# Row maxima of an attention kernel: head start of one and three quarter units instead of two

## The chip, the cores and the metric

The kernel runs on one core of one Trainium2 chip. The metric is the device time of one execution in microseconds (us), lower is better; of several executions the median counts.

## The reference

What is computed is one layer of gated cross attention and a gated, fake-quantised feed-forward part, on x of shape (8, 512, 256):

```python
x = x + tanh(g_xattn) * attention(layernorm(x), ctx, ctx)     # 16 heads of 16, rope on q and k, softmax
x = x + tanh(g_ffn) * ffn(layernorm(x))                       # 704 inner columns, int8 fake quantisation
```

The attention is the part that matters here: for each of 8 batches and 16 heads, scores = q k^T / 4 over 512 queries and 512 keys, a softmax over the keys, and the weighted sum of v. The softmax subtracts each query's largest score before the exponential.

## The kernel before

The program has three stages: projections and rope (stage A), attention (stage B), feed-forward (stage C). Each is a block in which the five engines run their own instruction streams and wait for one another by semaphores. The change touches stage B alone.

**Units and key tiles.** In stage B the work is cut in 32 units: batch b (8) times a group g of 4 heads. A unit has 4 key tiles kt of 128 keys. For each key tile and head h, TensorE computes the scores transposed (128 keys by 512 queries, `scores`, L716, four matmuls side by side) into one of three PSUM banks `st_ps`, and ScalarE takes the exponential of the bank (`exps`, L857). After the 4 heads of key tile kt, TensorE multiplies the probabilities of key tile kt-1 with the values (`weigh`, L748). At the second key tile of the next unit VectorE turns the finished sums (`turn_out`, L924) and inverts the denominators (`invert_sums`, L930).

**The row maxima come first.** A query's largest score must be known before its exponentials. It enters the score matmul as two more rows of q (a bf16 value and its rest) against rows of ones in k, so that the matmul itself subtracts it. To get it, the scores are computed once more the other way round, ahead of time: `query_scores` (L724) fills a pair of banks `mx_ps` with two query tiles of one head (8 matmuls), and VectorE's `maxima` (L916) reduces the pair to two columns of `negm`. A unit has 8 such pairs, and there are two pair buffers in turn. `ahead_scores` puts one pair behind the first and one behind the third head of every key tile (L809 to L812); so unit u+2's eight pairs are spread over the four key tiles of unit u: head kt of that unit at key tile kt. The first two units have nothing ahead of them: their 16 pairs stand alone in a prologue (L827 to L842 on TensorE, L1028 to L1036 on VectorE).

**How a maximum gets into q.** When a unit's eight pairs are read (`mx_read`), GpSimd splits `negm` in two bf16 parts (`split_max`, L1084 and L1086); TensorE turns them (`max_transpose`, L758) into a bank of the `st_ps` ring; ScalarE copies that to `mrow` (`take_max`, L862); and SyncE's queue sends two DMAs of 4 KB (`max_rows`, L688) into the two extra rows of `q6[g]`. TensorE waits for `mrow_in[g]` at the start of the unit (L806). `max_transpose` for unit u+1 stands behind the first key tile (kt == 0) of unit u, and so does `take_max`. SyncE's queue works strictly in order: at each unit first the 12 DMAs of `load_unit` (L184) for unit u+3, then `max_rows` for unit u+1.

**The ring of banks.** The 16 score tiles of a unit and the one turn of the maxima are 17 slots of a ring of three banks. `TURN_SLOT` says where in it the turn stands: at 4 (`HPU`), behind the fourth score tile. The slot three behind the turn waits for `mrow_ready`, the others for the exponential of the tile three slots before (`wait_score_bank`, L653).

```python
def slot(i):
    return i if i < TURN_SLOT else i + 1
```

**Other work in the stream.** In units g = 1 and 2 TensorE projects half of the previous batch's output behind key tile 1 (`project`, L795, in a pair buffer), and VectorE adds it at key tile 2 (`residual`, L945). In batch 0 VectorE also takes the weights' maxima, one per key tile (`weight_maxima`, L1000). ScalarE adds up moments of the result (L868, L874); in batches from 2 on, four key tiles in a row (g = 3, kt 2 and 3, then g = 0, kt 0 and 1) have one L874 each. The last batch has no unit two ahead for g = 2 and 3; there the pair buffers serve five jobs of weight transposes (`weight_transpose`, L770, four of 8 and one of 4; copied by `keep_weights`, L1025) at key tiles 0 to 4, `down_scales` (L778) at key tile 5, and VectorE's `x1_largest` (L961) at key tiles 0 to 5, counting the eight key tiles of the two units through.

Of the kernel before, what the change touches and what calls it, by code (L numbers as in the profile page):

```python
# [28 lines left out]
B, S, D = 8, 512, 256  # L29
# [4 lines left out]
TPB = S // P  # L34
KC = D // P
HPU = 4
# [49 lines left out]
def build(nc, a, scratch, out_dram):  # L86

    top = ExitStack()
    with top:
# [547 lines left out]

        TURN_SLOT = HPU  # L640
        PROJ_PAIR = (0, 1)

        def slot(i):

            return i if i < TURN_SLOT else i + 1

# [6 lines left out]
        def wait_score_bank(eng, b, g, i):  # L653

            n = 16 * (UPB * b + g)
            if slot(i) == TURN_SLOT + 3 and not (is_last(b) and g == 3):
                eng.wait_ge(mrow_ready, UPB * b + g + 2)
            elif i < 3:
                if not (is_first(b) and g == 0):
                    eng.wait_ge(exp_done, n - 16 + (14, 15, 13)[i] + 1)  # L660
            else:
                back = next(j for j in range(16) if slot(j) == slot(i) - 3) if slot(i) != TURN_SLOT + 3 else 1
                eng.wait_ge(exp_done, n + back + 1)

        def pair_bank(g, kt, j):

# [14 lines left out]
        with nc.Block() as block:  # L681
# [28 lines left out]
            def _(pe):  # L710
# [16 lines left out]

                def ahead_scores(b, g, kt, j):

                    mb, mg = (b, g + 2) if g < 2 else (b + 1, g - 2)  # L730
                    n = 8 * (UPB * mb + mg) + 2 * kt + j
                    if g in (1, 2) and kt == 2 and j == 1:
                        if not is_first(b):
                            pe.wait_ge(x1_ready, 2 * (b - 1) + g)
                    else:
                        pe.wait_ge(mx_read, n if g in (1, 2) and kt == 2 else n - 1)
                    query_scores(mb, mg, kt, j, pair_bank(g, kt, j))

                def weigh(b, g, kt):

# [11 lines left out]
                def max_transpose(b, g):  # L752

                    u = UPB * b + g
                    pe.wait_ge(msplit_ready, u + 2)
                    if g >= 0:
                        pe.wait_ge(exp_done, 16 * u + 2)
                    nc.tensor.transpose(turn_bank, msplit[(g + 1) % 2][:].rearrange("p n c -> p (n c)"), identb[:]).then_inc(maxT_ready, 1)  # L758

                jobs = [wfq[:, w * NIC + i, c * P:(c + 1) * P] for w in range(2) for c in range(KC) for i in range(NIC)]  # L760
# [20 lines left out]
                def project(b, hf):  # L781

                    dst = project_bank(b, hf)
                    pe.wait_ge(attnT_ready, 2 * b)
                    if is_tail(b):
                        pe.wait_ge(x1_ready, 2 * (B - 1))
                    elif is_last(b) and hf == 1:
                        pe.wait_ge(mx_read, 8 * NU)
                    else:
                        pe.wait_ge(mx_read, 8 * (UPB * b + hf + 3) + 3)  # L790
                    pe.wait_ge(woT_ready, 1)
                    for t in range(2):
                        for c in range(KC):
                            for lo in range(0, P, COLS):
                                last = nc.tensor.matmul(dst[lo:lo + COLS, t * D:(t + 1) * D], attnT[c][:, (2 * hf + t) * P + lo:(2 * hf + t) * P + lo + COLS], woT[:, c, :],  # L795
                                                        start=(c == 0), stop=(c == KC - 1), skip_group_check=True)
                    last.then_inc(wo_ready, 1)

                def body(b):
                    for g in range(UPB):  # L800
                        u = UPB * b + g
                        mb, mg = (b, g + 2) if g < 2 else (b + 1, g - 2)
                        ahead = not (is_last(b) and g >= 2)
                        if ahead:
                            pe.wait_ge(unit_in[mg], NLOAD * (mb + 1))
                        pe.wait_ge(mrow_in[g], MROWS * DMA * (b + 1))  # L806
                        for kt in range(TPB):

                            for h in range(HPU):  # L809
                                scores(b, g, kt, h)  # L810
                                if ahead and h in (0, 2):
                                    ahead_scores(b, g, kt, h // 2)  # L812
                            if kt:
                                weigh(b, g, kt - 1)
                            elif not (is_first(b) and g == 0):
                                weigh(*((b, g - 1) if g else (b - 1, 3)), 3)
                            if is_last(b) and g >= 2 and 4 * (g - 2) + kt < NWT:
                                weight_transpose(4 * (g - 2) + kt)
                            if is_last(b) and g == 3 and kt == 1:
                                down_scales()  # L820
                            if kt == 0 and not (is_last(b) and g == 3):
                                max_transpose(b, g)
                            if not is_first(b):
                                if kt == 1 and g in (1, 2):
                                    project(b, g - 1)

                for g in range(2):  # L827
                    pe.wait_ge(unit_in[g], NLOAD)
                    for h in range(HPU):
                        for j in range(2):  # L830
                            wait_if(pe, mx_read, 8 * g + 2 * h + j - 1)
                            query_scores(0, g, h, j, mx_ps[j])
                        if g == 0 and h >= 2:
                            c = h - 2
                            if c == 0:
                                pe.wait_ge(bv_ready, KC)
                            last = nc.tensor.matmul(wobv_ps, bv_rep[:, c, :], wo_raw[:, c, :], start=(c == 0), stop=(c == KC - 1))
                            if c == KC - 1:
                                last.then_inc(wobv_ready, 1)
                        if g and h == 0:  # L840
                            pe.wait_ge(bo_ready, 1)
                            max_transpose(0, -1)  # L842
# [6 lines left out]
            def _(act):  # L849
# [27 lines left out]
                def body(b):  # L877
                    for g in range(UPB):
                        for kt in range(TPB):
# [8 lines left out]
                            if beyond_second(b) and g == 0 and kt < 2:  # L888
                                x1_spread(b - 2, kt + 2)
                            exps(b, g, kt, (2, 3))  # L890
                            if kt == 0 and not (is_last(b) and g == 3):
                                take_max(b, g)
                for i in (0, 1):
                    mid_part(act, B - 1, i)
# [16 lines left out]
            def _(dve):  # L911
# [50 lines left out]

                def body(b):
                    for g in range(UPB):
                        mb, mg = (b, g + 2) if g < 2 else (b + 1, g - 2)
                        ahead = not (is_last(b) and g >= 2)
                        for kt in range(TPB):
                            if kt == 1 and not (is_first(b) and g == 0):
                                turn_out(b, g)
                            if kt == 2 and g in (1, 2) and not is_first(b):  # L970
                                residual(b, g - 1)
                            if ahead:
                                maxima(mb, mg, kt, 0, pair_bank(g, kt, 0))
                            if kt == 1 and not (is_first(b) and g == 0):
                                invert_sums(b, g)
                            if ahead:
                                maxima(mb, mg, kt, 1, pair_bank(g, kt, 1))
                            if kt == 3 and g == 0 and not is_first(b):
                                turn_back(b - 1, 1)
                            if kt == 3 and g == 2:  # L980
                                turn_back(b, 0)
                            if is_last(b) and g >= 2 and TPB * (g - 2) + kt < B - 2:
                                x1_largest(TPB * (g - 2) + kt)
                            if is_first(b):
                                weight_maxima(TPB * g + kt)
                            if is_last(b) and g >= 2 and 4 * (g - 2) + kt < NWT:
                                keep_weights(4 * (g - 2) + kt)
                            if is_last(b) and g == 3 and kt == 1:
                                dve.wait_ge(ds_ready, 1)
                                nc.vector.tensor_scalar(dscale[:], ds_ps, tanhg[:, 1:2], None, ALU.mult).then_inc(ds_read, 1)  # L990

# [39 lines left out]

                dve.wait_ge(wobv_ready, 1)
                nc.vector.tensor_tensor(bo_b[:], wobv_ps, bo_raw[:], ALU.add).then_inc(bo_ready, 1)
                for h in range(HPU):
                    for j in range(2):
                        maxima(0, 1, h, j, mx_ps[j])  # L1036
                dve.wait_ge(bo_ready, 1)
# [525 lines left out]
```

## Time and profile before

| | us |
|---|---|
| three executions | 617.42, 615.32, 617.26 |
| median | 617.26 |
| the profiled execution's own time | 615.77 |
| its span, first to last instruction | 614.0 |
| stage A, in the span | 0 to 107.5 |
| prologue of stage B (maxima of two units) | 107.6 to 127.3 |
| units of stage B | 127.3 to 502.4 |
| rest of stage B, and stage C | to 614.0 |

The profile is of one execution; its rows give the time from the span's start, and 1.8 us of the execution's time lie outside the span. PE is TensorE's matmul stream, PEld its weight loads, DVE VectorE, ACT ScalarE, POOL GpSimd and SPq the DMA queue of SyncE. PEclk is the granted TensorE clock as a share of 2.4 GHz.

### The profile page before, as it was taken

Reading aid. Unit: us, or ns where it says so; the run is one execution under the profiler, and the core shown is the slowest. Engines: PE = TensorE matmul, PEld = TensorE weight load, DVE = VectorE, ACT = ScalarE, POOL = GpSimd, SP = SyncE. Lnnn points to the kernel's source line nnn. Section 1 sums busy time; section 2 is a strip of 40 time slices with the busy share of each in tenths; the row PEclk is TensorE's granted clock in tenths of the full one; section 3 lists DMA queues with packets and bytes.
Section 4 is the critical chain, followed back from the end, with each engine's and each line's share of the span. In section 5 each row is a group of like instructions: output and inputs, shape, how many; then the busy total and the mean of one; then the engine's idle time right before and its main releaser. Section 6 shows DMA issues by size and latency. Waiting matters only on the chain. (4 is left out here: it accounts for less than half of the span.)

```text
span 614.0 us, 18320 instructions
## 1 busy us (share of the span) xinstructions
PE 554.1 (90%) x6473; PEld 259.5 (42%) x6478; DVE 531.4 (87%) x679; ACT 445.5 (73%) x886; POOL 263.9 (43%) x372
## 2 busy tenths in 40 slices
PE   6999997899899989999999999999999973988485
PEld 3555654244344424444444444444445321333264
DVE  3899989899999969899899899899899746689888
ACT  2667766247777867897897897897897771788694
POOL 7699996701233434214214314324323210899300
PEclk9999999569999989999999999999999997899889
DMA  8759877523432333242342243253240000000035
GB/s 291 238 164 294 242 203 203 154 55 68 81 65 64 77 61 63 55 89 63 57 89 62 59 86 63 60 85 61 62 90 8 2 2 1 0 2 0 0 104 172
DMA packets 61255, 55.20 MB, mean 90 GB/s; under 512 B 11040, under 2 KB 58784, under 8 KB 61216
## 3 DMA queue, kind: packets, MB, share of 16 engines
q1 hardware_dynamic: 61216, 54.70, 36.1%
q8 instruction: 22, 0.36, 0.2%
q14 instruction: 17, 0.14, 0.1%
HBM read 37.62 MB, written 16.78 MB: 89 GB/s over the span
## 5 line engine op out<-in xcount | busy, mean ns | idle before, releaser
L857 ACT ACTIVATE prob<-st_ps 128x512 f32<-128x512 f32 x512 | 281.2, 596 | 71.9 <-PE st_ps L716 64.9
L916 DVE TENSOR_REDUCE negm<-mx_ps 128x2 f32<-128x1024 f32 x256 | 300.1, 1206 | 17.6 <-PE mx_ps L724 17.4
L716 PE MATMUL st_ps<-q,k 98*32 98x512 bf16 x2048 | 182.5, 385 | 4.4 <-ACT prob L857 4.0
L724 PE MATMUL mx_ps<-k,q 96*32 96x512 bf16 x2048 | 164.8, 396 | 7.5 <-DVE negm L916 3.8
L748 PE MATMUL pv_ps<-prob,v_u 128*32 128x512 f32 x1024 | 133.7, 594 | 1.4 <-ACT prob L857 1.4
L716 PEld LDWEIGHTS st_ps<-q,k 98*32 98x32 bf16 x2048 | 58.6, 96 | 94.6 <-ACT prob L857 40.5
L724 PEld LDWEIGHTS mx_ps<-k,q 96*32 96x32 bf16 x2048 | 55.3, 98 | 79.3 <-DVE negm L916 25.5
L1084 POOL TENSOR_TENSOR msplit<-negm,onesf 128x16 bf16<-128x16 f32 x32 | 7.1, 221 | 135.6 <-DVE negm L916 125.7
L1104 POOL TENSOR_TENSOR normal<-turned,recip 128x256 f32<-128x256 f32 x32 | 19.9, 621 | 79.9 <-DVE recip L930 79.9
L748 PEld LDWEIGHTS pv_ps<-prob,v_u 128*32 128x32 f32 x1024 | 32.1, 111 | 27.3 <-ACT prob L857 3.0
L298 POOL TENSOR_TENSOR parts<-work 128x512 bf16<-128x512 f32 x32 | 38.4, 1206 | 7.1 <-DVE work L286 6.1
L1352 ACT ACTIVATE wf<-banks,gscale 128x512 f32<-128x512 f32 x44 | 30.0, 695 | 10.2 <-PE banks L1313 4.4
L1499 POOL TENSOR_TENSOR hst<-hq_even,wf 128x512 f32<-128x512 f32 x24 | 30.6, 1292 | 15.5 <-ACT hq_even L1358 15.2
L281 ACT ACTIVATE parts<-work 128x512 bf16<-128x512 bf16 x32 | 19.5, 625 | 23.2 <-DMA qk_parts<-parts 14.5
L387 PE MATMUL k_ps<-ctx,wk 128*128 128x512 f32 x64 | 31.1, 631 | 5.2 <-DMA ctx<-in_ctxT 5.2
L1094 POOL COPY v_u<-V 128x256 f32 (+1 forms) x32 | 12.7, 396 | 50.6 <-PE pv_ps L748 50.5
L795 PE MATMUL mx_ps<-woT,attnT 128*32 128x256 f32 x512 | 32.0, 394 | 2.6 <-DVE attnT L937 2.6
L262 POOL TENSOR_TENSOR work<-work 128x512 f32<-128x512 f32 x25 | 31.3, 1268 | 2.8 <-DVE work L257 2.7
L286 DVE TENSOR_TENSOR work<-work 128x512 f32<-128x512 f32 x30 | 29.2, 1011 | 3.0 <-POOL work L262 3.0
L411 PE MATMUL v_ps<-wv,ctx 128*128 128x256 f32 x128 | 29.1, 380 | 0.6 <-DMA wv<-in_wvT 0.6
L429 PE MATMUL q_ps<-xnT,wq 128*128 128x512 f32 x64 | 28.9, 595 | 0.5 <-ACT xnT L466 0.4
L445 ACT ACTIVATE xn<-X,shift,x_rstd 128x256 f32 (+1 forms) x32 | 16.6, 589 | 16.6 <-POOL shift L549 16.4
(126 smaller groups left out, 709.5 us busy)
## 6 DMA issues: line engine op xcount, KB each, us to landing
qk_parts<-parts SPq DMA_DIRECT2D x96, 128.0 KB, 2.8
k<-qk_parts SPq DMA_DIRECT2D x192, 64.0 KB, 2.8
q<-qk_parts SPq DMA_DIRECT2D x192, 64.0 KB, 2.9
ctx<-in_ctxT SPq DMA_DIRECT2D x8, 512.0 KB, 4.5
X<-in_x SPq DMA_DIRECT2D x8, 512.0 KB, 7.7
out<-X SPq DMA_DIRECT2D x7, 512.0 KB, 2.9
q<-mrow SPq DMA_DIRECT2D x64, 4.0 KB, 2.5
wf<-in_w_down SPq DMA_DIRECT2D x1, 704.0 KB, 5.0
```

Source lines behind the costliest of these rows:

```text
L262: ns.tensor_tensor(work[:, i, 0, :], work[:, i, 0, :], work[:, i, 1, :], ALU.add if i % 2 else ALU.subtract)\
L286: ns.tensor_tensor(work[:, i, 1, :], work[:, i, 0, :], top_half(work[:, i, 0, :]), ALU.subtract).then_inc(r1_ready, 1)
L298: nc.gpsimd.tensor_tensor(parts[:, i, 2, :], work[:, i, 1, :], top_half(work[:, i, 1, :]), ALU.subtract).then_inc(lo_ready, 1)
L387: last = nc.tensor.matmul(k_ps[:, m, :], wk[:, c, m * P:(m + 1) * P], ctx[odd][:, c, :], start=(c == 0), stop=(c == KC - 1))
L716: last = nc.tensor.matmul(score_bank(i)[lo:lo + COLS, :], k6[g][:, h, kt * P + lo:kt * P + lo + COLS], q6[g][:, h, :], start=True, stop=True)
L724: last = nc.tensor.matmul(pair[lo:lo + COLS, qt % 2, :], q6[g][0:ROWS, h, qt * P + lo:qt * P + lo + COLS], k6[g][0:ROWS, h, :], start=True ...
L748: last = nc.tensor.matmul(pv_ps[32 * h:32 * h + 32, :], v_u[g % 2][:, kt, h, :], prob[kt % 2][:, h, :], start=(kt == 0), stop=(kt == TPB - 1))
L795: last = nc.tensor.matmul(dst[lo:lo + COLS, t * D:(t + 1) * D], attnT[c][:, (2 * hf + t) * P + lo:(2 * hf + t) * P + lo + COLS], woT[:, c, :],
L857: nc.scalar.activation(prob[kt % 2][:, h, :], score_bank(HPU * kt + h)[:], ACT.Exp, scale=SCALE).then_inc(exp_done, 1)
L916: nc.vector.tensor_reduce(negm[g % 2][:, lo:lo + 2], pair[:], op=ALU.max, axis=AX.X, negate=True).then_inc(mx_read, 1)
L1352: nc.scalar.activation(sil[s % UR], g_ps[s % GR], ACT.Silu, scale=gscale[:, c:c + 1]).then_inc(sil_ready, 1)
L1499: nc.gpsimd.tensor_tensor(hst[:, bass.ds(SLOTS * p + s, 1), :].rearrange("p o t -> p (o t)"), upb[j % UBR], sil[s % UR], ALU.mult).then_in ...
```

## The change

The maxima of a unit now begin one key tile later. Key tile 0 of unit u serves the last head (3) of unit u+1, and key tiles 1, 2 and 3 serve heads 0, 1 and 2 of unit u+2. The prologue has 14 pairs, all 8 of unit 0 and the first 6 of unit 1. The turn of the maxima, and ScalarE's copy of it, stand behind the second key tile instead of the first, and `TURN_SLOT` is 8. In the last batch the pairs go on for one key tile longer (g = 2, kt = 0), and the weight transposes, `x1_largest` and `down_scales` stand one key tile later. The counts in the waits are shifted to match; TensorE's wait for the loaded q and k of the unit ahead moves from the unit's start to its key tile 1.

```diff
-        TURN_SLOT = HPU
+        TURN_SLOT = 2 * HPU
...
-                back = next(j for j in range(16) if slot(j) == slot(i) - 3) if slot(i) != TURN_SLOT + 3 else 1
+                back = next(j for j in range(16) if slot(j) == slot(i) - 3) if slot(i) != TURN_SLOT + 3 else TURN_SLOT - 3
                 eng.wait_ge(exp_done, n + back + 1)
+
+        def ahead_unit(b, g, kt):
+
+            g2 = g + (2 if kt else 1)
+            return (b, g2) if g2 < UPB else (b + 1, g2 - UPB)
+
+        def is_ahead(b, g, kt):
+
+            return not is_last(b) or g < 2 or (g == 2 and kt == 0)
...
-                    mb, mg = (b, g + 2) if g < 2 else (b + 1, g - 2)
-                    n = 8 * (UPB * mb + mg) + 2 * kt + j
+                    mb, mg = ahead_unit(b, g, kt)
+                    n = 8 * (UPB * b + g) + 14 + 2 * kt + j
...
-                    query_scores(mb, mg, kt, j, pair_bank(g, kt, j))
+                    query_scores(mb, mg, (kt + 3) % 4, j, pair_bank(g, kt, j))
...
-                        pe.wait_ge(exp_done, 16 * u + 2)
+                        pe.wait_ge(exp_done, 16 * u + TURN_SLOT - 2)
...
-                        pe.wait_ge(mx_read, 8 * (UPB * b + hf + 3) + 3)
+                        pe.wait_ge(mx_read, 8 * (UPB * b + hf + 3) + 1)
...
-                        if ahead:
-                            pe.wait_ge(unit_in[mg], NLOAD * (mb + 1))
                         pe.wait_ge(mrow_in[g], MROWS * DMA * (b + 1))
                         for kt in range(TPB):
-
+                            ahead = is_ahead(b, g, kt)
+                            if ahead and kt == 1:
+                                mb, mg = ahead_unit(b, g, kt)
+                                pe.wait_ge(unit_in[mg], NLOAD * (mb + 1))
...
-                            if is_last(b) and g >= 2 and 4 * (g - 2) + kt < NWT:
-                                weight_transpose(4 * (g - 2) + kt)
-                            if is_last(b) and g == 3 and kt == 1:
+                            if is_last(b) and 0 < 4 * (g - 2) + kt <= NWT:
+                                weight_transpose(4 * (g - 2) + kt - 1)
+                            if is_last(b) and g == 3 and kt == 2:
                                 down_scales()
-                            if kt == 0 and not (is_last(b) and g == 3):
+                            if kt == 1 and not (is_last(b) and g == 3):
                                 max_transpose(b, g)
...
-                        for j in range(2):
+                        for j in range(2 if g == 0 or h < HPU - 1 else 0):
                             wait_if(pe, mx_read, 8 * g + 2 * h + j - 1)
                             query_scores(0, g, h, j, mx_ps[j])
...
-                            if kt == 0 and not (is_last(b) and g == 3):
+                            if kt == 1 and not (is_last(b) and g == 3):
                                 take_max(b, g)
...
-                for h in range(HPU):
+                for h in range(HPU - 1):
                     for j in range(2):
                         maxima(0, 1, h, j, mx_ps[j])
```

VectorE's loop is changed in the same way as TensorE's (the head and unit of each `maxima`; `x1_largest`, `keep_weights` and the product `dscale` one key tile later).

## Rows read from the trace of the kernel before

**Rows 1.** The page, part 1: busy time and share of the span.
```profile
PE 554.1 (90%) x6473; PEld 259.5 (42%) x6478; DVE 531.4 (87%) x679; ACT 445.5 (73%) x886; POOL 263.9 (43%) x372
```
**Rows 2.** Windows: length, busy of PE, PEld, DVE, ACT, POOL, then PEclk, DMA, GB/s.
```profile
107.60:127.30 19.70, 17.37 (x137) 3.92 (x137) 17.73 (x16) 3.93 (x7) 10.79 (x17) 0.53 0.53 137
...
142.00:178.00 36.00, 33.25 (x500) 14.51 (x496) 35.19 (x48) 27.39 (x54) 7.42 (x17) 1.00 0.34 70
...
316.00:474.00 158.00, 157.96 (x2446) 68.96 (x2442) 145.81 (x153) 132.08 (x288) 50.07 (x94) 1.00 0.34 66
```
**Rows 3.** Timeline of the prologue: start, us, engine, line, operation.
```profile
119.27 9.49 DVE L916 TENSOR_REDUCE negm<-mx_ps 128x2 f32<-128x1024 f32 x8 [0.29 <-PE mx_ps L724]
...
121.61 1.23 SPq L688 DMA_DIRECT2D q<-mrow  x2
...
127.27 0.64 PE L716 MATMUL st_ps<-q,k 98*32 98x512 bf16 x4
```
**Rows 4.** Timeline of units (7,0) and (7,1).
```profile
453.98 0.40 PE L716 MATMUL st_ps<-q,k 98*32 98x512 bf16 x4
...
454.86 2.35 DVE L916 TENSOR_REDUCE negm<-mx_ps 128x2 f32<-128x1024 f32 x2 [0.46 <-PE mx_ps L724]
...
456.58 0.22 PE L758 MATMUL st_ps<-identb,msplit 128*32 128x128 bf16 x1
...
458.45 1.03 PE L748 MATMUL pv_ps<-prob,v_u 128*32 128x512 f32 x8
...
458.79 3.19 ACT L857 ACTIVATE prob<-st_ps 128x512 f32<-128x512 f32 x6
...
464.51 0.40 PE L716 MATMUL st_ps<-q,k 98*32 98x512 bf16 x4
```
**Rows 5.** Tile mrow, whole span: the DMAs, ScalarE's copy, and the landing times.
```profile
L688 SPq DMA_DIRECT2D q<-mrow x64: 502/579/843, 121.6 to 480.8; - x64
L862 ACT ACTIVATE mrow<-st_ps x32: 250/250/268, 120.2 to 480.0; 32x128 bf16<-32x128 bf16 x32
...
DMA to landing us min/median/max: 1.6/2.5/4.4
```
**Rows 6.** Tile mrow, 118 to 126 us: the landing of the prologue's two DMAs.
```profile
DMA to landing us min/median/max: 1.8/1.8/1.9
```
**Rows 7.** Lines of 127 to 490 us: GpSimd's second split instruction.
```profile
L1086 POOL TENSOR_TENSOR msplit<-negm,msplit 128x16 bf16<-128x16 f32 x31 | 6.7, 217 | 2.4
```
**Rows 8.** Windows around the prologue's end; columns as in rows 2.
```profile
127.20:129.00 1.80, 1.80 (x24) 0.52 (x20) 1.80 (x4) 0.60 (x1) 0.00 (x0) 0.50 0.62 159
...
132.00:134.00 2.00, 2.00 (x32) 1.24 (x28) 1.74 (x3) 1.43 (x4) 0.00 (x0) 0.87 0.02 4
```
**Rows 9.** Timeline of the last batch: a key tile with pairs.
```profile
471.78 0.64 PE L724 MATMUL mx_ps<-k,q 96*32 96x512 bf16 x8
...
474.38 0.64 PE L724 MATMUL mx_ps<-k,q 96*32 96x512 bf16 x8
```
**Rows 10.** The same timeline, g = 2 and 3: the key tiles without pairs.
```profile
487.44 0.83 PE L716 MATMUL st_ps<-q,k 98*32 98x512 bf16 x12
...
490.29 0.83 PE L716 MATMUL st_ps<-q,k 98*32 98x512 bf16 x12
...
492.91 1.50 PE L716 MATMUL st_ps<-q,k 98*32 98x512 bf16 x16
...
495.21 0.71 PE L778 MATMUL mx_ps<-diag,onesf 128*128 128x128 f32 x4
495.85 0.83 PE L716 MATMUL st_ps<-q,k 98*32 98x512 bf16 x12
...
496.30 1.08 ACT L857 ACTIVATE prob<-st_ps 128x512 f32<-128x512 f32 x2 [0.87 <-PE st_ps L716]
...
498.04 1.75 PE L716 MATMUL st_ps<-q,k 98*32 98x512 bf16 x16
...
500.16 1.12 ACT L857 ACTIVATE prob<-st_ps 128x512 f32<-128x512 f32 x2
```

More of the change, by code:

```diff
@@ L801, in body @@
                         u = UPB * b + g
-                        mb, mg = (b, g + 2) if g < 2 else (b + 1, g - 2)
-                        ahead = not (is_last(b) and g >= 2)
-                        if ahead:
-                            pe.wait_ge(unit_in[mg], NLOAD * (mb + 1))
                         pe.wait_ge(mrow_in[g], MROWS * DMA * (b + 1))
                         for kt in range(TPB):
+                            ahead = is_ahead(b, g, kt)
+                            if ahead and kt == 1:
+                                mb, mg = ahead_unit(b, g, kt)
+                                pe.wait_ge(unit_in[mg], NLOAD * (mb + 1))
                             for h in range(HPU):
@@ L964, in body @@
                     for g in range(UPB):
-                        mb, mg = (b, g + 2) if g < 2 else (b + 1, g - 2)
-                        ahead = not (is_last(b) and g >= 2)
                         for kt in range(TPB):
+                            mb, mg = ahead_unit(b, g, kt)
+                            ahead = is_ahead(b, g, kt)
                             if kt == 1 and not (is_first(b) and g == 0):
@@ L972, in body @@
                             if ahead:
-                                maxima(mb, mg, kt, 0, pair_bank(g, kt, 0))
+                                maxima(mb, mg, (kt + 3) % 4, 0, pair_bank(g, kt, 0))
                             if kt == 1 and not (is_first(b) and g == 0):
@@ L976, in body @@
                             if ahead:
-                                maxima(mb, mg, kt, 1, pair_bank(g, kt, 1))
+                                maxima(mb, mg, (kt + 3) % 4, 1, pair_bank(g, kt, 1))
                             if kt == 3 and g == 0 and not is_first(b):
@@ L981, in body @@
                                 turn_back(b, 0)
-                            if is_last(b) and g >= 2 and TPB * (g - 2) + kt < B - 2:
-                                x1_largest(TPB * (g - 2) + kt)
+                            if is_last(b) and 0 < TPB * (g - 2) + kt <= B - 2:
+                                x1_largest(TPB * (g - 2) + kt - 1)
                             if is_first(b):
                                 weight_maxima(TPB * g + kt)
-                            if is_last(b) and g >= 2 and 4 * (g - 2) + kt < NWT:
-                                keep_weights(4 * (g - 2) + kt)
-                            if is_last(b) and g == 3 and kt == 1:
+                            if is_last(b) and 0 < 4 * (g - 2) + kt <= NWT:
+                                keep_weights(4 * (g - 2) + kt - 1)
+                            if is_last(b) and g == 3 and kt == 2:
                                 dve.wait_ge(ds_ready, 1)
```

## The prediction

> **What bounds the kernel now.** I read the page's first part, then busy time by stretch, then the timeline at the four places that the change touches. On the page TensorE has 90% and VectorE 87% of the span [rows 1]; the averages don't say who is last in which stage, the stretches do. In 316 to 474 us TensorE's busy time is 157.96 of 158.00 us, VectorE's 145.81: the units are bound by TensorE [rows 2]. In batch 0 (142 to 178 us), where VectorE also has the weights' maxima, it is the other way round: VectorE 35.19 of 36.00 us, TensorE 33.25 [rows 2]. In the prologue VectorE reads eight pairs in 9.49 us without a gap, 1.186 us for a pair [rows 3]; TensorE only refills what VectorE has freed. The prologue's pairs come before the first score tile, at 127.27 us [rows 3], so the prologue costs VectorE's time, while ScalarE is busy 3.93 of 19.70 us there [rows 2].
>
> **Part 1, two pairs leave the prologue.** TensorE's first score tile stands behind the issue of the last pair, and that waits for the read two pairs before. With 14 pairs instead of 16 it stands 2 x 1.186 = **2.37 us** earlier, at 124.90. What else must be there by then: the two row DMAs of unit 0. They are issued at 121.61 us, SyncE's queue being the one that lets them go; the turn behind them keeps its place, so this time stays. The second is issued 0.62 us later (half of 1.23) and lands 1.9 us on at the latest [rows 3, 6], at 124.13: 0.77 us to spare. The q and k of units 0 and 1 are waited for inside the prologue as before. From there batch 0 does the same work in the same order and, being limited by VectorE's stream, keeps the 2.37 us.
>
> **Part 2, the pairs run as before in the units.** 256 pairs before, 256 after; key tile 0 has another unit's head, with equal shapes. A key tile with pairs takes 474.38 - 471.78 = 2.60 us [rows 9]. Nothing is added: 0.
>
> **Part 3, the turn moves from key tile 0 to 1.** Its instructions are the same: two on GpSimd, one turn, one copy, two DMAs. What changes is how early each input is there and how soon the result is needed. I take unit (7,0), one of the short ones without a projection (10.53 us, from 453.98 to 464.51) [rows 4]. The input: VectorE has read key tile 0's second pair at 454.86 + 2.35 = 457.21. GpSimd's two splits of 0.22 us each [rows 7] with some 0.3 us of hand-over give 458.0. The turn will be asked for behind this unit's weigh of key tile 1, at 458.45 + 1.03 = 459.48 [rows 4]. Cover 1.5 us, so no wait; without it TensorE, with all score tiles of key tiles 2 and 3 queued behind, stands still. The bank: the turn needs the exponentials two before the last, which are done; the next tiles need the last two of key tile 1, done by 458.79 + 2 x 0.53 = 459.85 by today's stream, when the second tile behind the turn starts at about 459.96. That is close, but ScalarE no longer has the 0.25 us copy in front of them [rows 5], so they end earlier. I take 0, bounds 0 to 0.2 us in the eight units with g = 0. The result: the copy ends at some 460.1, the DMAs are issued at 460.2 and 460.75 (0.58 us each), and with the median landing of 2.5 us the rows are in q at 463.25 [rows 5]. They are needed at 464.51. Cover 1.26 us. In units with g = 1 and 2 a projection stands behind the turn, so the cover is larger. SyncE's queue: the 12 load DMAs stay ahead of the rows; today the rows go out as soon as that queue gets to them, now as soon as the copy is there, and nothing is queued behind them until the next unit's scores are issued. Sum of part 3: 0.
>
> **Part 4, the last batch.** Before, from g = 2, kt = 0 on, key tiles carry weight transposes and no pairs. Tiles with a full job take 490.29 - 487.44 = 2.85 us, the one with the half job 492.91 - 490.29 = 2.62, the one with the down scales 495.85 - 492.91 = 2.94, the next one, empty, 498.04 - 495.85 = 2.19 [rows 10]. After: one tile with pairs (2.60) comes first, and the others follow one place later. Up to the start of the third key tile of g = 3 there are then four full, one half and one with pairs, where there were four full, one half and one with down scales: 2.60 - 2.94 = **-0.34 us**. The down scales come into the tile that was empty. There ScalarE sets the end: from 496.30 it works to 500.16 + 1.12 = 501.28 with exponentials and moment sums queued [rows 10], so the 0.75 us (2.94 - 2.19) should lie beside that. I take it as hidden; bound +0.75, which makes part 4 between -0.34 and +0.41.
>
> **Part 5, TensorE's clock.** From the prologue through 132 us the granted clock is 0.50, that is 1.2 GHz, and it goes back to 2.4 GHz inside 132 to 134 us (0.87 there) [rows 8]: with 0.87 = 1 - 0.5 x d / 2, d = 0.52, at 132.5. The prologue's TensorE is busy 17.37 of 19.70 us [rows 2] without getting it; the rise comes 5.3 us after the dense matmuls begin at 127.27. I take it that it follows the dense stretch and moves with it: 0. If it comes at the same moment as before, the 2.37 us won are run at half speed and half is lost, 1.19 us. If it comes sooner behind the dense stretch, at most some 0.5 us are won.
>
> The Trainium skill (TensorE: Matmul & The Clock Gate, Part 1) says that the warm-up is a budget of time under sustained activity and not a number of matmuls, which would move the rise along with the start, and also that its moment varies from run to run. By that rule the sum stays as it is. That 17.37 busy us of the prologue's 19.70 [rows 2] don't earn the rise is what this trace adds to it.
>
> **Sum.** -2.37 + 0 + 0 - 0.34 + 0 = -2.71 us. Against the profiled execution's own 615.77 us that gives 613.06. That execution is 1.49 us below the median of the three runs, 617.26; the difference taken from the median gives **614.55 us**, 0.44% faster. 0.5%, about what a measurement of this kernel can tell from no change, is 3.1 us: the forecast lies just inside it.
>
> **Rivals.**
> A, the clock. The rise stays at 132.5: -2.71 + 1.19 = -1.5, 615.7 us. For it: the clock ignored the prologue's 20 us. Against: rows 8 show a rise after dense work only.
>
> B, the first scores wait for unit 0's rows instead. A landing as in the worst row, 4.4 us [rows 5] instead of 1.9, puts it at 126.63, so 1.73 of the 2.37 us go and -1.0 is left: 616.3 us. Against: both landed within 1.9 [rows 6], and the queue that gates them is unchanged.
>
> C, slower: the rows come late in each short unit. Half of the units have no projection; in batch 0 there is room, so 14 count. Break-even per unit is a landing of 2.5 + 1.26 = 3.76 us; the kernel is 3.1 us slower than before when each loses (3.1 + 2.7) / 14 = 0.41 us, a landing of 4.2 us. At the longest landing, 4.4, each loses 0.64: 9.0 - 2.7 = +6.3, 623.5 us. For it: the head start after the turn has shrunk by a key tile, 2.60 us. Against: the median landing is 2.5 [rows 5], and the rows now leave when the load DMAs before them have had a microsecond more to drain.
>
> D, no effect on the prologue's end because something else, such as the loads, gates the first tiles: only the -0.34 is left, 616.9 us. Against: VectorE's eight reads have no gap.
>
> **Chances.** Forecast 0.69, A 0.12, B 0.05, C 0.07, D 0.07. The forecast's own range comes from the bounds (-2.7 - 0.5 to -2.7 + 0.75 + 0.2 x 8 = 1.6 at the very most) and from the runs shown, which lie between 1.9 us below and 0.2 above their median: 612.3 to 616.2. To hold A and B it goes to 617.0. Faster by over 0.5% is about half of the forecast's case, for its centre is 0.4 us short of the line: 0.35. Slower by over 0.5% is C: 0.07. The rest is 0.58.
>
> **What would show it.** VectorE's run of eight reads ahead of the first score tile shrinks to six, with the first L716 at about 124.9 us and the clock's rise some 5 us after it. Units of g = 0 and 3 of the same 10.5 us, with no wait of TensorE for GpSimd or a DMA at their ends. In the last batch the down scales at the third key tile of g = 3, and ScalarE's exponentials behind them without a longer gap. Wrong it would be if short units grew (C), or if the span up to the second unit shrank by less than 2 us (A, B, D).

## The result, and the profile after

| | before | after |
|---|---|---|
| median of 22 executions each | 615.65 us | 614.14 us |
| lowest, highest | 614.09, 618.62 | 611.15, 616.41 |
| the profiled execution | 615.77 | 615.11 |
| its span | 614.0 | 613.2 |

The ratio of the times is 0.9968 with a 95% interval of 0.9955 to 0.9981: 2.0 us less, by the interval 1.2 to 2.8; the two medians alone differ by 1.5 us. The forecast was 2.71 us less. The measured time lies inside the range, and the change stays within 0.5%.

In the kernel after, the score matmul is L725, the pairs' matmul L733, the weigh L757, the turn L767, ScalarE's copy L870, the row DMAs L697, VectorE's read L924, GpSimd's split L1092 and the down scales L787. First the timeline of its prologue (start, length, engine, line); it answers to [rows 3].

```profile
120.37 7.11 DVE L924 TENSOR_REDUCE negm<-mx_ps 128x2 f32<-128x1024 f32 x6 [0.29 <-PE mx_ps L733]
120.95 0.31 PE L767 MATMUL st_ps<-identb,msplit 128*32 128x128 bf16 x1
...
121.77 1.23 SPq L697 DMA_DIRECT2D q<-mrow  x2
...
125.98 0.64 PE L725 MATMUL st_ps<-q,k 98*32 98x512 bf16 x4
```

Six reads stand behind the turn instead of eight. From the first of them to the first score tile it is 125.98 - 120.37 = 5.61 us; before it was 127.27 - 119.27 = 8.00. The difference, 2.39 us, is the two pairs. The start of the first score tile moved by only 1.29, and here a reader can be misled: in this execution stage B began 0.67 us later (its first pair, L733, at 108.29 instead of L724 at 107.62), and from there to the read at 120.37 it took 0.43 us more. Its first pairs had the fast clock (2.4 GHz) for less than 0.1 us; in the profile before they had it for 1.0 us. Neither has to do with the change: e1, which has the old prologue, shows the longer of the two stretches as well (12.09 us), and e7, which is the changed kernel again, the shorter (11.66).

Next the timeline of units (7,0) and (7,1), which answers to [rows 4].

```profile
452.29 0.40 PE L725 MATMUL st_ps<-q,k 98*32 98x512 bf16 x4
...
455.60 0.22 POOL L1092 TENSOR_TENSOR msplit<-negm,onesf 128x16 bf16<-128x16 f32 x1 [7.68 <-DVE negm L924]
...
456.62 1.04 PE L757 MATMUL pv_ps<-prob,v_u 128*32 128x512 f32 x8
...
457.48 0.22 PE L767 MATMUL st_ps<-identb,msplit 128*32 128x128 bf16 x1
...
457.92 0.25 ACT L870 ACTIVATE mrow<-st_ps 32x128 bf16<-32x128 bf16 x1
...
458.19 1.15 SPq L697 DMA_DIRECT2D q<-mrow  x2
...
462.81 0.40 PE L725 MATMUL st_ps<-q,k 98*32 98x512 bf16 x4
```

GpSimd has split the maxima by 456.1, TensorE turns them at 457.48, behind the weigh, and no wait stands in that row; the rows leave at 458.19. The unit takes 462.81 - 452.29 = 10.52 us, as before (10.53). The landing times of tile mrow over the whole span answer to [rows 5]:

```profile
DMA to landing us min/median/max: 1.6/2.0/3.2
```

and 316 to 474 us by windows to [rows 2] (busy PE, PEld, DVE, ACT, POOL, then PEclk):

```profile
316.00:474.00 158.00, 157.96 (x2451) 70.11 (x2447) 145.94 (x153) 133.06 (x287) 49.70 (x94) 1.00 0.34 65
```

TensorE's 157.96 is the same number. From (2,1) on, all units up to (7,2) start 1.70 to 1.72 us earlier than in the profile before: nothing is gained or lost over 240 us.

The last batch, timeline of g = 3, answers to [rows 10].

```profile
493.96 0.83 PE L725 MATMUL st_ps<-q,k 98*32 98x512 bf16 x12
...
496.25 0.71 PE L787 MATMUL mx_ps<-diag,onesf 128*128 128x128 f32 x4
496.89 0.83 PE L725 MATMUL st_ps<-q,k 98*32 98x512 bf16 x12
...
497.35 1.09 ACT L865 ACTIVATE prob<-st_ps 128x512 f32<-128x512 f32 x2 [0.39 <-PE st_ps L725]
```

The third key tile of g = 3, which was 2.19 us and has the down scales now, takes 496.89 - 493.96 = 2.93 us, and ScalarE waits 0.39 us behind it. I had taken it as hidden. All eight key tiles of (7,2) and (7,3), from the starts of their first score tiles in the two timelines; the last one is counted to the start of the last weigh:

```
          (7,2) kt 0   1     2     3    (7,3) kt 0   1     2     3
before        2.85   4.86  2.84  2.84       2.62   2.94  2.19  3.29
after         2.59   4.72  2.87  2.84       2.84   2.89  2.93  3.05
```

From (7,2)'s start to the last weigh it was 501.33 - 476.90 = 24.43 us and is 499.94 - 475.20 = 24.74: 0.31 us longer, where I forecast 0.34 shorter.

**The sum of the two profiled executions** up to the last weigh: stage A and the first pairs +1.10, the two pairs -2.39, the clock in unit 0 -0.97 and what unit (0,1) gives back of it +0.26, units (1,3) and (2,0) with their clock +0.28, the last batch +0.31: together -1.41, and the last weigh is 1.39 us earlier. Behind the last weigh the span goes on for 112.6 us before and 113.3 us after. The change doesn't touch that part, and it differs as much between other executions: 112.4 us in e5, 113.3 in e7. What I put down to the change itself is -2.39 + 0.31 = -2.08 us, and the 44 executions say -2.0.

### The profile page after: what moved, and what is told of

Its sections match the earlier page's. It is cut to its first block and busy times, and to the rows that moved or that the text cites. A ratio compares the mean times of both kernels' runs of the same rounds, so it can differ in the third digit from the quotient of the medians.

```text
span 613.2 us, 18348 instructions
## 1 busy us (share of the span) xinstructions
PE 553.9 (90%) x6478; PEld 260.2 (42%) x6478; DVE 530.8 (87%) x679; ACT 448.2 (73%) x886; POOL 262.8 (43%) x372
## 5 line engine op out<-in xcount | busy, mean ns | idle before, releaser
L924 DVE TENSOR_REDUCE negm<-mx_ps 128x2 f32<-128x1024 f32 x256 | 300.1, 1206 | 18.0 <-PE mx_ps L733 17.9
L725 PE MATMUL st_ps<-q,k 98*32 98x512 bf16 x2048 | 180.7, 383 | 4.6 <-ACT prob L865 4.5
L733 PE MATMUL mx_ps<-k,q 96*32 96x512 bf16 x2048 | 163.8, 395 | 6.8 <-DVE negm L924 3.2
L757 PE MATMUL pv_ps<-prob,v_u 128*32 128x512 f32 x1024 | 133.4, 595 | 1.5 <-ACT prob L865 1.4
L1092 POOL TENSOR_TENSOR msplit<-negm,onesf 128x16 bf16<-128x16 f32 x32 | 7.1, 221 | 214.4 <-DVE negm L924 214.4
L725 PEld LDWEIGHTS st_ps<-q,k 98*32 98x32 bf16 x2048 | 58.2, 96 | 94.2 <-ACT prob L865 37.9
L733 PEld LDWEIGHTS mx_ps<-k,q 96*32 96x32 bf16 x2048 | 54.3, 98 | 83.3 <-DVE negm L924 27.8
L757 PEld LDWEIGHTS pv_ps<-prob,v_u 128*32 128x32 f32 x1024 | 31.5, 110 | 27.9 <-ACT prob L865 3.9
L1381 ACT ACTIVATE wf<-hst,ainv 128x1024 int16<-128x1024 f32 (+1 forms) x24 | 23.8, 1066 | 6.2 <-DVE ainv L1401 4.3
```

Of the source, the lines that this page charges most:

```text
L725: last = nc.tensor.matmul(score_bank(i)[lo:lo + COLS, :], k6[g][:, h, kt * P + lo:kt * P + lo + COLS], q6[g][:, h, :], start=True, stop=True)
L733: last = nc.tensor.matmul(pair[lo:lo + COLS, qt % 2, :], q6[g][0:ROWS, h, qt * P + lo:qt * P + lo + COLS], k6[g][0:ROWS, h, :], start=True ...
L757: last = nc.tensor.matmul(pv_ps[32 * h:32 * h + 32, :], v_u[g % 2][:, kt, h, :], prob[kt % 2][:, h, :], start=(kt == 0), stop=(kt == TPB - 1))
L924: nc.vector.tensor_reduce(negm[g % 2][:, lo:lo + 2], pair[:], op=ALU.max, axis=AX.X, negate=True).then_inc(mx_read, 1)
```

## The experiments

Ten runs were made, e7 of them with the changed kernel as it is. Those with a single execution (e2, e4, e6) are read by the stretches of their profile, since executions of one kernel lie up to 7 us apart.

**e1, the turn alone.** The kernel before, with the turn one key tile later and nothing else.

```diff
-        TURN_SLOT = HPU
+        TURN_SLOT = 2 * HPU
...
-                            if kt == 0 and not (is_last(b) and g == 3):
+                            if kt == 1 and not (is_last(b) and g == 3):
                                 max_transpose(b, g)
```

> The kernel before with only the turn of the maxima and its copy moved from key tile 0 to key tile 1 (16 pairs in the prologue, last batch as before). My theory: the move is free, every unit keeps its length (10.53 us for g = 0 in batches 3 to 7, 12.3 for g = 1 and 2), no wait of TensorE for GpSimd or a DMA at a unit's end; time within 0.1% of before, 615.6 us. Rival, rows late: the units with g = 0 and 3 grow by 0.4 us or more, +6 us in all.

Measured: 615.35 us against 616.17, ratio 0.9989 (0.9964 to 1.0014), no difference that shows; by time alone that leaves room for 2 us less or 1 us more. In its profile all units from (2,1) to (7,1) keep their length within 0.02 us, and 316 to 474 us reads

```profile
316.00:474.00 158.00, 157.96 (x2454) 70.06 (x2446) 145.86 (x153) 133.13 (x288) 50.05 (x94) 1.00 0.34 66
```

Its prologue from the ninth read to the first score tile takes 8.00 us, as before. Its rows landed in 1.6 to 3.6 us, 2.1 in the median: with the turn's move alone they land sooner than the 2.5 of before. So the turn's move costs nothing that the units show, and the prologue's gain belongs to the two pairs.

**e2, the turn where it was.** The changed kernel with `TURN_SLOT = HPU` and both conditions back at `kt == 0`: it shows what the move of the turn is for.

> The changed kernel with the turn left behind key tile 0, as before the change, while the maxima it needs are computed in that same key tile. My theory: TensorE reaches the turn 1.4 us before GpSimd's split is ready (maxima read at 457.21 in unit (7,0), split by 457.9 to 458.0, turn asked for at 456.58), so units where TensorE is the bound lose about 1 to 1.4 us each: 27 units, +25 to +40 us against the changed kernel, some 640 to 655 us. Rival: the reorder of the weight loads and the ring of banks absorb it, under 5 us.

Measured: 664.03 us in one execution, 50 more than the changed kernel's 614.14. Its waits between 127 and 540 us (who waited for whom, us in total, times, longest):

```profile
ACT mrow L870 <- PE st_ps L767: 43.7, 31, 2.1
PE st_ps L767 <- POOL msplit L1094: 41.1, 31, 1.7
```

and its timeline in unit (7,0):

```profile
498.52 0.22 POOL L1092 TENSOR_TENSOR msplit<-negm,onesf 128x16 bf16<-128x16 f32 x1 [7.96 <-DVE negm L924]
498.82 0.22 POOL L1094 TENSOR_TENSOR msplit<-negm,msplit 128x16 bf16<-128x16 f32 x1
...
499.09 0.23 PE L767 MATMUL st_ps<-identb,msplit 128*32 128x128 bf16 x1 [1.11 <-POOL msplit L1094]
```

In the steady batches key tile 0 takes 4.18 to 4.40 us instead of 2.61, and whole units take 1.45 to 1.65 us more (g = 0 has 11.98 instead of 10.53). TensorE's wait itself is 41.1 / 31 = 1.3 us for each turn, inside the 1 to 1.4 I expected. The rest of a unit's loss, 0.1 to 0.3 us, the four units that I hadn't counted and 2 us behind the last weigh make the total of 50 where I wrote 25 to 40. ScalarE waits 1.4 us for each turn as well and has no tiles meanwhile; that the rest comes from this is not shown.

**e3, the down scales behind the last weigh.** The changed kernel; TensorE issues them where it waits for VectorE, and VectorE multiplies them behind its last `turn_back`.

```diff
-                            if is_last(b) and g == 3 and kt == 2:
-                                down_scales()
...
                 weigh(B - 1, 3, 3)
+                down_scales()
```

> The changed kernel with the down scales taken out of the last unit's third key tile and put behind the last weigh, where TensorE waits 2.6 us for VectorE. My theory: the 0.74 us by which that key tile grew (2.93 instead of 2.19 us) come back, of which 0.5 had reached the end of stage B: the stretch from unit (7,2)'s first score tile to the last weigh falls from 24.74 to some 24.2 us; 0.5 us less in all, about 0.1%. Rival, it was hidden all the same: the stretch stays within 0.1 us of 24.74.

Measured: the third key tile is 2.19 us again, and the stretch from (7,2) to the last weigh 24.25 us, 0.5 less than in the changed kernel. Time 614.34 us, ratio to before 0.9966 (0.9943 to 0.9989), which alone can't tell 0.5 us. The stretch is as expected: of the 0.74 us by which the key tile had grown, 0.5 had reached the end.

**e4, the down scales late, in the kernel before.** `kt == 1` becomes `kt == 2`, alone.

> The kernel before with the down scales alone moved one key tile later, g = 3, kt = 2. My theory: the old place costs 2.94 - 2.19 = 0.75 us, the new place costs the same 0.75 and the relief at the old one is paid back: the stretch from unit (7,2)'s first score tile to the last weigh stays at 24.43 us within 0.15. Rival, as I predicted: the new place is covered by ScalarE's queue and the stretch falls by 0.5 to 0.75 us, to 23.7 to 23.9.

Measured: 24.17 us instead of 24.43, so 0.26 less, which fits neither statement. Its key tiles say where: 2.94 falls to 2.19, 2.19 grows to 2.92, and the last one shrinks from 3.29 to 3.05. A quarter of a microsecond of the later place is covered, the other half microsecond is not. Both theories were too simple: the cover is 0.25 us, not nothing and not 0.75. The rows of the profile before show how much cover there is.

```profile
497.76 2.06 ACT L857 ACTIVATE prob<-st_ps 128x512 f32<-128x512 f32 x4
498.04 1.75 PE L716 MATMUL st_ps<-q,k 98*32 98x512 bf16 x16
```

TensorE begins the last key tile's scores at 498.04. ScalarE could take up the first of them 0.45 us later, at 498.49 (in the timelines of g = 3 its exponentials, when it waits for them, start 0.45 to 0.46 us behind the score tile). It is free for it when two of its four exponentials from 497.76 are done, at 498.79. So TensorE is 0.3 us ahead, an estimate from these rows; whatever comes in on top of it makes ScalarE wait, 0.39 us in the changed kernel.

**e5, a prologue without gaps.** The changed kernel with four more matmuls, whose result nobody reads, behind each of the 14 pairs.

```diff
                             query_scores(0, g, h, j, mx_ps[j])
+                            for lo in range(0, P, COLS):
+                                nc.tensor.matmul(st_ps[0][lo:lo + COLS, :], q6[0][0:ROWS, 0, lo:lo + COLS], k6[0][0:ROWS, 0, :], start=True, stop=True)
```

> The changed kernel with one more group of four score matmuls, whose result nobody reads, behind each of the prologue's 14 pairs, so that TensorE has no gaps there. My theory, that the gaps hold the clock at 1.2 GHz through the prologue and that this costs the first key tiles of unit 0: the granted clock is back at 2.4 GHz well inside the prologue, unit 0's first two key tiles take 5.3 us or less instead of 5.95 (and up to 7.25 in e3), and the span up to unit (0,1) is 0.5 to 2 us shorter. Rival, the clock isn't gained by density: it stays at 1.2 GHz, each prologue pair then takes 1.28 us instead of 1.19, the first score tile comes 1.3 us later and the kernel is 1 us slower.

Measured: 614.25 us, ratio to before 0.9985 (0.9957 to 1.0013), the same as the changed kernel. Windows of its profile (length, busy PE, PEld, DVE, ACT, POOL, then the granted clock):

```profile
108.00:112.00 4.00, 4.00 (x52) 1.22 (x44) 3.61 (x4) 1.54 (x4) 4.00 (x6) 0.57 0.33 88
112.00:116.00 4.00, 3.52 (x54) 1.18 (x50) 4.00 (x4) 1.15 (x3) 3.88 (x4) 1.00 0.44 114
116.00:120.00 4.00, 3.54 (x47) 1.07 (x39) 4.00 (x5) 0.89 (x2) 2.52 (x8) 1.00 0.70 200
120.00:124.00 4.00, 2.56 (x40) 0.68 (x36) 4.00 (x5) 0.00 (x0) 0.00 (x0) 1.00 0.67 194
124.00:128.00 4.00, 1.38 (x16) 0.57 (x20) 1.10 (x2) 0.60 (x1) 0.00 (x0) 0.68 0.28 64
```

The same four stretches in the changed kernel:

```profile
112.00:116.00 4.00, 3.71 (x26) 0.78 (x18) 3.98 (x4) 1.26 (x2) 3.92 (x5) 0.50 0.65 142
116.00:120.00 4.00, 4.00 (x27) 1.20 (x30) 3.10 (x4) 0.63 (x1) 2.88 (x8) 0.50 0.74 221
120.00:124.00 4.00, 3.35 (x29) 0.59 (x21) 3.69 (x5) 0.27 (x1) 0.26 (x2) 0.50 0.56 161
124.00:128.00 4.00, 3.89 (x36) 1.07 (x40) 3.98 (x5) 0.64 (x2) 0.00 (x0) 0.50 0.39 92
```

In this execution the clock is back at 2.4 GHz by 112 us, as expected. The gain was not there, and two rows of its timeline show rival B as the reason:

```profile
122.44 1.23 SPq L697 DMA_DIRECT2D q<-mrow  x2
126.62 0.62 PE L725 MATMUL st_ps<-q,k 98*32 98x512 bf16 x4 [3.17 <-DMA q<-mrow]
```

TensorE has issued its last pair by 123.5 and then waits 3.17 us for the rows of unit 0. ScalarE's copy had ended at 119.42, but the rows stand in SyncE's queue behind twelve stores to `qk_parts` until 122.4, and landed up to 3.5 us after their issue. In that idle stretch, at 125.4 us, the clock falls again, and unit 0's first key tiles take 3.39 and 3.70 us. From the first pair to unit (0,1) it is 31.25 us, against 28.85 and 28.98 in the two profiles of the changed kernel.

That the gaps are what holds the clock down is not shown by this. In e10 the same groups stand behind the first eight pairs, and the clock comes back at 123.2 us only; in e6, with no unread matmul at all, it comes back at 118.8.

**e6, one step further.** 12 pairs in the prologue, the turn behind key tile 2, all counts shifted by two again.

```diff
-        TURN_SLOT = 2 * HPU
+        TURN_SLOT = 3 * HPU
...
-            g2 = g + (2 if kt else 1)
+            g2 = g + (2 if kt >= 2 else 1)
```

> The changed kernel one step further the same way: 12 pairs in the prologue, maxima one and a half units ahead, the turn behind key tile 2. My theory: the prologue loses 2.37 us more, but now the rows are the last to arrive. In a unit with g = 0 the copy ends some 8.6 us after the unit's start, the second DMA is issued 0.7 us later and lands 2.5 us on, at 11.8 against 10.5 needed: 1.3 us lost; with g = 1 and 2 the copy ends at 10.3, the landing is at 13.5 against 12.3. In all 30 to 45 us slower than the changed kernel, 640 to 660 us. Rival, the chain is shorter than I count and the gain simply goes on: 612 us.

Measured: 632.81 us in one execution, 18 more than the changed kernel instead of 30 to 45. Its first score tile waits 1.12 us for unit 0's rows (rival B again), so from the first pair to it there are 16.03 us instead of 17.69: 1.7 of the further 2.37 us. In steady batches g = 0 takes 10.8 us instead of 10.5, g = 1 and 2 lose 0.3 each, and g = 3 takes 12.5 instead of 10.7. Its timeline in unit (2,3) and the start of (3,0):

```profile
270.81 0.22 POOL L1092 TENSOR_TENSOR msplit<-negm,onesf 128x16 bf16<-128x16 f32 x1 [8.45 <-DVE negm L924]
...
271.63 0.62 POOL L1112 TENSOR_TENSOR normal<-turned,recip 128x256 f32<-128x256 f32 x1
...
272.36 0.20 POOL L150 TENSOR_TENSOR mean<-x_sum,ln_const 128x4 f32 x1
272.70 0.51 ACT L882 ACTIVATE unused<-X,negmean 128x256 bf16 x1 [1.38 <-POOL mean L150]
...
273.83 0.40 PE L725 MATMUL st_ps<-q,k 98*32 98x512 bf16 x4 [1.40 <-ACT prob L865]
...
276.88 0.40 PE L725 MATMUL st_ps<-q,k 98*32 98x512 bf16 x4 [0.27 <-DMA q<-mrow]
```

The last line is rival C as I had written it: a unit's first score tile waits for its rows, 0.27 us here and 8.4 us over 25 such tiles. The rows landed sooner than I priced, 1.7 us in the median instead of 2.5, which is most of why it is not 1.3. The larger part at this place, 1.4 us, is one I had not listed: GpSimd's queue is in order, the split now waits for later maxima, and the small means behind it (L150), for which ScalarE waits, come late with it. So one step of this kind is free and two are not.

**e7, the changed kernel again**, on the chip of e5, e6 and e8.

> The changed kernel as it is, for comparison on the same chip: 614.1 us, 0.3% below before. In its profile the steady units keep 10.53, 12.3, 12.3 and 10.7 us for g = 0 to 3, the last batch's stretch from unit (7,2) to the last weigh takes 24.7 us, and only the stage before and the clock's changes differ from the first profile, by 1 us or less each.

Measured: 614.44 us, ratio 0.9979 (0.9954 to 1.0004): the size of the first result, and an interval that just takes in no change. First read behind the turn to first score tile 5.62 us, stretch from (7,2) to the last weigh 24.75 us, steady units as in the first profile: the three findings repeat. Unit 0's first two key tiles take 3.41 and 3.09 us here (3.14 and 2.81 in the first profile), unit (1,3)'s last one 7.40 (6.32): these are the parts that differ from execution to execution.

**e8, weight transposes inside the key tile.** e3, and `weight_transpose` issued ahead of the fourth score tile instead of behind the weigh.

```diff
                             for h in range(HPU):
+                                if h == 3 and is_last(b) and 0 < 4 * (g - 2) + kt <= NWT:
+                                    weight_transpose(4 * (g - 2) + kt - 1)
                                 scores(b, g, kt, h)
```

> e3 (down scales behind the last weigh) and, besides, the weight transposes of the last batch put between the third and the fourth score tile, where TensorE waits 0.27 us for a bank, instead of behind the weigh. My theory: a key tile with a full job then takes 2.4 instead of 2.85 us, because ScalarE's exponentials go on meanwhile; four of them and a half one give 1.5 to 2 us, and the stretch from unit (7,2) to the last weigh falls from 24.25 (e3) to 22.3 to 22.8 us; the time to some 612.0 us. Rival: it only moves the wait, stretch 24.0 or more.

Measured: 611.13 us, ratio 0.9925 (0.9900 to 0.9951). The stretch falls to 22.04 us, key tiles with a full job from 2.84 to between 2.44 and 2.58. They had been a loop of waits: in each of them TensorE waited 0.27 us for ScalarE, and ScalarE up to 0.78 us for TensorE.

**e9, the means first.** e8, and in unit (1,3) GpSimd's means ahead of the 4.03 us preparation of the weights.

> e8 and, besides, GpSimd's two small means of batch 0's result (L149, L150) put ahead of the 4.03 us preparation of the weights in unit (1,3), instead of behind it. My theory: ScalarE waits 3.5 us for these means there, which makes key tile 3 of unit (1,3) 6.3 to 7.4 us long; it falls to about 2.8, and the TensorE clock no longer drops behind it. 3.5 to 5 us less than e8: 606 to 607.5 us, 1.4% below before. Rival, the preparation then delays the next unit's split and the wait only moves: 610 us or more.

The waits of the changed kernel from 200 to 240 us have

```profile
ACT unused L882 <- POOL mean L150: 3.5, 1, 3.5
PE st_ps L725 <- ACT prob L865: 2.7, 1, 2.7
```

and e9's timeline shows the new order:

```profile
212.85 0.20 POOL L149 TENSOR_TENSOR negmean<-x_sum,ln_const 128x4 f32<-128x4 f32 x1
213.01 0.20 POOL L150 TENSOR_TENSOR mean<-x_sum,ln_const 128x4 f32<-128x4 f32 x1
213.17 4.03 POOL L1129 TENSOR_SCALAR wfq<-wf 128x4608 bf16<-128x4608 f32 x1
213.33 0.61 PE L733 MATMUL mx_ps<-k,q 96*32 96x512 bf16 x8
213.69 0.50 ACT L881 ACTIVATE unused<-X,negmean 128x256 bf16<-128x256 f32 x1
```

Measured: 606.46 us, ratio 0.9844 (0.9817 to 0.9871), 1.6% below before. The key tile takes 2.72 us, the next unit has 10.53 instead of 11.63, and the granted clock stays at 1.00 there (it was 0.50 from 222 to 224 us in the changed kernel).

**e10, e9 with a denser prologue**: one unread group behind each of unit 0's pairs, two behind each of unit 1's.

> e9 with unread score matmuls in the prologue again, one group of four behind each of unit 0's pairs and two behind each of unit 1's (e5 had one each, and the clock fell back at 125.4 us). My theory: with the second group the clock holds at 2.4 GHz up to the first score tile, unit 0's first two key tiles take 5.3 us or less, and the kernel is 0.3 to 1 us faster than e9. Rival: VectorE sets the pace there anyway, within 0.3 us of e9.

Measured: 608.37 us, ratio 0.9881 (0.9856 to 0.9905). The clock does hold from 123.2 us on, and unit 0's first two key tiles take 2.05 and 3.38 us, but the first score tile comes later: by the profiles 2.84 us, of which 1.17 lie ahead of the first pair, and 1.67 in the prologue. Until 123.2 the unread matmuls ran at half clock and stood in front of the pairs. It doesn't pay. Its windows:

```profile
112.00:116.00 4.00, 4.00 (x37) 1.36 (x30) 3.83 (x4) 1.38 (x3) 3.92 (x5) 0.50 0.60 120
116.00:120.00 4.00, 4.00 (x27) 1.44 (x27) 2.61 (x3) 0.63 (x1) 2.91 (x7) 0.50 0.62 175
120.00:124.00 4.00, 4.00 (x43) 1.45 (x46) 2.65 (x4) 0.10 (x1) 0.44 (x2) 0.60 0.69 202
```

TensorE has no recorded gap there, and its clock stays at 1.2 GHz to 123.2 us all the same.

## Why the prediction was right

**Part 1, the two pairs:** forecast -2.37, measured -2.39, and -2.38 in e7. The rows of unit 0 were in time, as their landing had said [rows 6]; rivals B and D fall for this kernel. B is the next limit, though: e5 and e6 both ran into it.

**Part 2 and 3, pairs and turn in the units:** forecast 0, measured 0 in the steady units, by the changed kernel and by e1 alone. The copy ended 5.9 us behind the unit's start (I had 6.1), and the landing was 2.0 us in the median where I had taken 2.5. Rival C needed 4.2. The landing is shorter now, and in e1 too, so it goes with the turn's move; that the load DMAs drain first is argued, not tested apart.

**Part 4, the last batch:** forecast -0.34, measured +0.31; the step that failed. Two terms of it were mis-sized. The pair tile for the tile with down scales gave -0.19 instead of -0.34 up to the third key tile of g = 3. The half job now stands at a key tile 1, whose weigh starts at 492.64, just behind VectorE's turn (491.78 to 492.48): 2.89 us and not 2.62; the tile with the projection, 4.72 instead of 4.86, gives half of that back. And "hidden" was wrong for the down scales: 0.5 of 0.75 us came through, e3 gives them back, e4 shows the cover to be 0.25. I had read rightly that ScalarE works from 496.30 to 501.28 without a gap. But an engine without a gap covers extra work of the other only as far as that other is ahead of it, and here TensorE was ahead by 0.3 us, as worked out under e4. The bound, +0.41, held.

**Part 5, the clock:** I took 0 with a gain of up to 0.5. In the first profile the clock came back 2.85 us behind the first score tile instead of 5.26, worth 0.97 us there, of which unit (0,1) gave 0.26 back: 0.7 us net, more than my bound. It is not the change's, though. e3 and e7, whose code is the same up to there, have unit 0's first two key tiles at 3.41 + 3.84 and 3.41 + 3.09 us, with the rise 5.9 and 4.4 us behind the first score tile, and e1, with the prologue of before, has it after 3.5. So the moment differs from one execution to the next, as the Trainium skill says (TensorE: Matmul & The Clock Gate, Part 1). Rival A, a rise fixed at 132.5 us, falls with the first profile, where it came at 128.8.

The sum that the change makes is -2.08 where -2.71 was forecast; the interval holds both. That the time came within 0.4 us of the forecast, 614.14 against 614.55, is partly luck: the forecast starts from 617.26, the median of three executions, and the median of 22 is 615.65. From there it would have been 612.94, 1.2 us too low. The forecast's own range, 612.3 to 616.2, doesn't follow from its terms either: -3.2 and -0.35 from 617.26, with the spread of the runs, make 612.2 to 617.1. The measured time lies in both.

## What to carry to other kernels

When work moves out of a prologue, first ask which engine's stream sets the prologue's end: the gain is that engine's time for the moved part, and it survives if the place it goes to has none of it on the path. "Hidden beside another engine" wants the lead of the one over the other at that place, from the start of a piece of work to the moment when the next engine is free for it: an engine that is busy without a gap covers no more than that lead. And an in-order queue that is made to wait for a later result delays everything small behind it: look there before taking the same step twice.

## What the runs showed beyond the expectation

TensorE was busy 3.35 to 4.00 us of every four in the prologue at a granted clock of 0.50. With one more group of matmuls for each pair the clock was at 1.00 by 112 us in one profile (e5); in another, with the same groups behind the first eight pairs, it stayed at 0.50 to 123.2 us, though TensorE was recorded busy without a gap (e10); and in e6, without any, it was back at 118.8 us and gone again at 122.2. Over whole executions the mean granted clock is 0.959 to 0.975 in e5 and 0.968 to 0.975 in e10, against 0.950 to 0.966 in e7 and 0.958 to 0.969 in e9. So more matmuls in the prologue bring more time at the fast clock on the whole, but busy time in such rows doesn't say when the clock will rise, and what decides it stays open. And the largest find had nothing to do with the change: two instructions of 0.20 us behind one of 4.03 us in GpSimd's queue cost 4 to 5 us at one place (key tile 6.40 to 2.72 and next unit 11.55 to 10.53 between the profiles of e8 and e9), more than twice what the change brought.
